# Second attention layer of a two-layer gated network: the inverse standard deviations by one GpSimd power instead of VectorE's Newton steps

## The reference, cut to what matters

```
def _layernorm(x, eps=1e-05):
    m, v = mean(x), var(x)                 # over the 256 features of a token
    return (x - m) / sqrt(v + eps)
...
x = x + tanh(g_ffn[0])   * _L0_ffn_ref(_layernorm(x), ...)                # 64 experts
x = x + tanh(g_xattn[1]) * _L1_xattn_ref(_layernorm(x), ctx, ctx, mask, ...)   # "first" norm
x = x + tanh(g_ffn[1])   * _L1_ffn_ref(_layernorm(x), ...)                # "second" norm
```

## Time and profile before

| what | value |
|---|---|
| time, median of 3 runs | 2185.94 us (2185.69 to 2190.29) |
| span of the profiled execution | 2056.7 us |
| what lies between that span and the median | 129.2 us |
| busy, share of the span: TensorE, VectorE, ScalarE, GpSimd | 90%, 77%, 60%, 44% |
| second attention layer in the trace | about 1138 to 1841 us |

### The profile page before, as it was taken

The page is one execution under the profiler, slowest core; times in us unless marked ns, Lnnn a source line. Parts: engine busy times, 40 slices in busy tenths (PEclk is TensorE's granted clock), DMA queues, the critical chain, the costliest instruction groups (busy, mean ns, idle before and its releaser), DMA issues.

```text
span 2056.7 us, 58130 instructions
## 1 busy us (share of the span) xinstructions
PE 1843.9 (90%) x21352; PEld 1494.5 (73%) x21488; DVE 1577.7 (77%) x6201; ACT 1236.8 (60%) x2555; POOL 902.1 (44%) x844
## 2 busy tenths in 40 slices
PE   4999999999999996499999699999999999958856
PEld 3898888888888885388888477777777777733334
DVE  4899999999999998444444677777777777769976
ACT  3676676676676672122222466666666666648877
POOL 1276666666666667577777100000000000005468
PEclk8999999999999998699999899999999999989978
DMA  9831221221111112499998211111111111003264
GB/s 233 224 117 57 58 60 51 62 77 47 50 51 45 49 36 79 133 224 213 219 218 151 63 40 40 40 40 40 41 35 38 40 40 41 17 24 154 93 243 166
DMA packets 183321, 187.69 MB, mean 91 GB/s; under 512 B 36946, under 2 KB 165749, under 8 KB 180992
## 3 DMA queue, kind: packets, MB, share of 16 engines
q1 hardware_dynamic: 135520, 142.30, 22.1%
q0 software_dynamic: 47520, 41.67, 11.0%
HBM read 103.33 MB, written 140.77 MB: 119 GB/s over the span
## 4 chain that ended last, share of the span: by engine, by line
PE 46%; DVE 32%; issue 9%; DMA 7%; POOL 3%; ACT 1%; SPq 1%; POOLq 0%; DVEq 0%; ACTq 0%
PE bank L423 11%; PE tiles L354 6%; DMA accumulator<-ye,tid 6%; DVE mt L786 6%; PE tiles L336 4%; PE bank L386 3%; PE bank L438 3%; PE tiles L330 2%; PE tiles L348 2%; DVE hmax L1610 2%; PE bank L458 2%; POOL accumulator L1400 2%; PE bank L469 2%; DVE h_ring L1603 2%; PE bank L371 2%
## 5 line engine op out<-in xcount | busy, mean ns | idle before, releaser
L1912 POOL DMA_INDIRECT expert_rows<-pay,idx x512 | 504.7, 986 | 246.0 <-issue 172.2
L1926 POOL TENSOR_TENSOR res<-res,bias 128x256 f32<-128x256 f32 x64 | 46.5, 726 | 611.9 <-ACT xn L629 611.9
L786 DVE TENSOR_REDUCE mt<-tiles 128x8 f32<-128x1024 f32 x256 | 300.8, 1216 | 8.4 <-PE tiles L336 8.2
L587 ACT ACTIVATE pt<-tiles 128x2048 f32<-128x2048 f32 x128 | 244.3, 1909 | 7.7 <-PE tiles L354 7.7
L609 ACT ACTIVATE qkp<-bank,qb,keep 128x128 f32<-128x128 f32 x512 | 209.3, 471 | 51.9 <-PE bank L423 51.9
L1400 POOL DMA_INDIRECT accumulator<-ye,tid x128 | 198.7, 1552 | 87.1 <-DMA accumulator<-ye,tid 38.2
L609 ACT ACTIVATE qkp<-bank,kb,keep 128x128 f32<-128x128 f32 x500 | 207.1, 482 | 0.0
L423 PE MATMUL bank<-xt,w_q 128*128 128x128 f32 x1024 | 164.5, 284 | 1.0 <-ACT xt L595 1.0
L354 PEld LDWEIGHTS tiles<-qm,qkp 32*128 32x128 f32 x4096 | 125.8, 186 | 52.4 <-issue 27.0
L354 PE MATMUL tiles<-qm,qkp 32*128 32x128 f32 x4096 | 150.2, 283 | 10.6 <-DVE mt L786 3.7
L336 PE MATMUL tiles<-qkp 32*128 32x128 f32 x4096 | 152.6, 285 | 6.2 <-ACT qkp L609 6.2
(11 more groups left out here) (265 smaller groups left out, 4289.4 us busy)
## 6 DMA issues: line engine op xcount, KB each, us to landing
expert_rows<-zt POOLq DMA_DIRECT2D x16, 1032.0 KB, 10.0
xr<-expert_rows SPq DMA_DIRECT2D x64, 258.0 KB, 4.2
cxax<-in_ctx SPq DMA_DIRECT2D x128, 128.0 KB
cxax<-accumulator SPq DMA_DIRECT2D x128, 128.0 KB, 2.2
hidden_away<-h_ring SPq DMA_DIRECT2D x8, 1536.0 KB, 5.1
res<-in_x SPq DMA_DIRECT2D x64, 128.0 KB
accumulator<-xa SPq DMA_DIRECT2D x64, 128.0 KB, 1.8
accumulator<-zt SPq DMA_DIRECT2D x64, 128.0 KB
```

What stands on the lines that cost most here:

```text
L587: nc.scalar.activation(pt[r % 2][:, :, :], tiles[:, :, :], ACT.Exp).then_inc(sem(sm("exp_done")), 1)
L786: last = nc.vector.tensor_reduce(mt[:, j, :].rearrange("p (i e c) -> p i e c", i=RT, e=2)[:, :, :, 0], tiles[:, :, 2 * j * P:2 * (j + 1) * ...
L1912: G.indirect_dma_start(out=xe[:, :], out_offset=bass.IndirectOffsetOnAxis(ap=idx[r][:, n:n + 1], axis=0), in_=pay[r][:, :], in_offset=None ...
```

## The change

For the second layer `NORM_STEPS` becomes 3. VectorE writes `var`, goes on to `shifted(m)`, and then waits for GpSimd's step before it writes `nmr`. GpSimd's loop gets, ahead of each bias addition, a wait for `var`, the two waits that guard `rstd` (formerly VectorE's), and one `tensor_tensor` with the operation `pow` of 128x2 elements that writes `rstd` = var to the power of -0.5. The loop runs six turns longer (70 in place of 64) to serve the last blocks' second norm. The first layer keeps its 13 steps.

```
-    NORM_STEPS = 13
+    NORM_STEPS = (13, 3)
...
+        minus_half = sb("minus_half", [P, 2])
...
-                act.wait_ge(sem(sm("rstd_step")), NORM_STEPS * (b + 1))
+                act.wait_ge(sem(sm("rstd_step")), NORM_STEPS[L] * (b + 1))
...
-                act.wait_ge(sem(sm("rstd_step")), NORM_STEPS * (b + PAIR[L] + 1))
+                act.wait_ge(sem(sm("rstd_step")), NORM_STEPS[L] * (b + PAIR[L] + 1))
...
                 st.mark(V.tensor_scalar(var[:, :], mv[:, :, 1], EPS, None, ALU.add))
                 yield
+                if L == 1:
+                    dve.wait_ge(sem("rstd_step_1"), NORM_STEPS[1] * s1 + 2)
+                    nc.vector.scalar_tensor_tensor(nmr[:, :], mv[:, :, 0], -1.0, rstd[:, :], ALU.mult, ALU.mult
+                                                   ).then_inc(sem("rstd_step_1"), 1)
+                    return
...
-                    norming(11)
+                    norming(1)
                     shifted(m)
-                    norming(2)
+                    norming(1)
...
+            G.memset(minus_half[:, :], -0.5)
...
-            for b in range(NB):
-                pool.wait_ge(sem("xn1_done_1"), b + 1)
-                G.tensor_tensor(row(b), row(b), bias[:, :], ALU.add).then_inc(sem("biased_1"), 1)
+            for s in range(NB + PAIR[1]):
+                pool.wait_ge(sem("rstd_step_1"), NORM_STEPS[1] * s + 1)
+                wait(pool, "xn1_done_1", min(s, NB))
+                wait(pool, "xn2_done_1", s - PAIR[1])
+                G.tensor_tensor(rstd[:, :], var[:, :], minus_half[:, :], ALU.pow).then_inc(sem("rstd_step_1"), 1)
+                if s < NB:
+                    pool.wait_ge(sem("xn1_done_1"), s + 1)
+                    G.tensor_tensor(row(s), row(s), bias[:, :], ALU.add).then_inc(sem("biased_1"), 1)
```

More of the change, by code:

```diff
@@ L861, in inverses @@
                 V = nc.vector
-                st = Steps(dve, sm("rstd_step"), NORM_STEPS, s1)
+                st = Steps(dve, sm("rstd_step"), NORM_STEPS[L], s1)
                 dve.wait_ge(sem(sm("stats_done")), s1 + 1)
```

## The result

The changed kernel takes 2179.29 us (2171.91 to 2182.55, 5 runs) against 2188.35 us (2185.69 to 2190.29, 5 runs) of the kernel before beside it: a ratio of 0.9948, interval 0.9929 to 0.9967. The forecast was 2177.9 us, 8.04 us less than before; the medians differ by 9.1 us, and 0.52% of 2188 us is 11.4 us, with 7 to 16 us by the interval. So the timed runs show that there is a gain and about how large it is; which part of the phase it comes from is read from the traces. One of the later timed runs of the changed kernel (c1_after) took 3695.0 us where the others took 2185 to 2199, and is left out of its ratio.

The account below looks back on a forecast made before the run. The prediction took TensorE to bound the full slots and latency the two ends. Filling 3.66 plus draining 4.38 us gave 8.04 us, so 2185.94 became 2177.9 us, with a range of 2173.5 to 2186.5 us.

Parts of the forecast that it names:

- The power's time: The 128x2 power on GpSimd, called p: taken as 0.6 us, with bounds of 0.12 and 2.77 us.
- 3q: Three times the gain of one bare chain, q = 2.04 - p = 1.44 us, within the sum 3.72 + 3q.
- The hops: Handing over from VectorE to GpSimd and back: 0.08 us each way, 0.16 us together.
- bare chain: Newton steps from `var` to `nmr` at the pipeline's ends, where TensorE has nothing: 2.20 us, each to gain 1.44 us.
- Filling: Start of the phase: first chain 1.44, wait for block 1's `xn` 0.61, second maximum 1.61; together 3.66 us gained.
- Full slots: The 59 middle slots: power hidden in slack, gain taken as 0, with 2.95 us as the other end.
- Draining: End of the phase: slot 65's wait for `qm` 1.18, head sums 0.32, two bare chains 2.88; together 4.38 us gained.
- what lies outside the span: Whole execution: 129.2 us between the profiled span and the measured median were said to lie outside and stay.
- start-up cost: Rival in the filling stretch: the first power runs code not run before, adding an extra L once; chance 0.05.
- the ends were not hidden: Denies the rival that expert-sum loads or feed-forward weights hold the chains at the ends: 2183 to 2186 us, chance 0.05.
- the power did not block VectorE's `qm`: Denies the rival that `shifted` (0.88 us) starts only when the power ends; its chance is within the slow power's 0.14.
- The slow power: Rival: a power over 2.71 us delays each full slot one for one; at 4 us some 2264 us; chance 0.14.

Follow-up runs that it names:

- e7: Changed kernel with the token maximum moved from between head norm and residual to the start of the slot; ratio 0.9934 to the kernel before.
- e9: Changed kernel with the token maximum at slot start and the second layer's copy of the values moved from ScalarE to VectorE; ratio 0.9914 to the kernel before.
- e1: Kernel before, all Newton steps still on VectorE, with only the order changed: `shifted` right behind `var`, the other twelve instructions after it; ratio 0.9992.
- e4: Changed kernel with the power kept, but VectorE waits for it ahead of `shifted`, undoing the new order; ratio 0.9936 to the kernel before.
- c0_before: Kernel before, unchanged, run again for a trace from an execution of known device time; ratio 0.9987.
- e3: Changed kernel with four spare GpSimd powers per call, each awaited, ahead of the one that counts; ratio 1.0314 to the kernel before.
- e6: Changed kernel with the power in the first layer too, on GpSimd behind each block's second scatter transfer; ratio 1.0173 to the kernel before.

## Why the prediction was right, and where it was off

**The power's time.** 0.6 us taken, 0.70 measured. This was a guess inside bounds of 0.12 and 2.77 us and not a derivation, and that it came so close is partly luck: the term 3q moves by three times its error. The prediction also counted ten instructions as removed from VectorE; it is eleven, which changes no term, since the chain was priced by its 2.20 us. The hops were 0.16 together by forecast; by the trace 0.15 and 0.03 in the fill, 0.07 and 0.04 in the drain. A bare chain gained 1.29 us in the fill and 1.40 in the drain, against 1.44.

**Filling**, 3.66 forecast, 4.2 between the two profiled executions. The first chain gave 1.29; L403 of block 1 came 2.10 us earlier, so that wait gave 0.81 for 0.61; the scores of block 1 came 2.56 us earlier and the second maximum 4.18, so the wait behind the Newton steps gave 1.62 for 1.61. The 0.46 us between 2.10 and 2.56 are mostly the clock: the first L336 took 2.09 us before and 1.68 after. TensorE's granted clock in this stretch differs between executions of one kernel, and the fill with it: 25.9 and 26.6 us before, 20.8 and 21.7 after. The 1 us kept open was the right size; it went either way.

**Full slots**, 0 forecast; 10.53 us a slot in both traces of before, 10.52 and 10.53 in the two of after, so nothing clear of scatter. Right in size. The reason given was incomplete: "the middle is TensorE's", and "ScalarE is no bound for it", which was read at `xn` alone. e7 shortened TensorE's wait at L372 and the slot did not move; e9 took 0.17 us out of ScalarE's round besides (5.21 to 5.04 us from L610 to the end of `copy_at`) and it did. The slot is a ring over both: in e7 5.1 us of TensorE from L387 to the end of L424 and 5.2 us of ScalarE from L610 to the end of `copy_at`, with two hops of 0.04 and 0.14 us. TensorE's 97% hid that, since it fills the ring's other half with work of its own. This was the step that failed in the reading, though it cost the forecast nothing.

**Draining**, 4.38 forecast; slot 65 gave 1.25 (1.18 forecast) and the tail 3.28 (0.32 + 2.88 forecast), together 4.53. The attribution was wrong in one term: 1.18 us were booked to the new place of `shifted`, but e1 shows the place alone worth nothing in sum and e4 the power alone worth 4.3. Slot 64 then took back 2.7 us in the one trace by the lower clock, which hit the kernel before in c0_before as well. What decides between the levels there stays open: the idle time before it is 2.5 to 2.6 us in each case (2.60 before and 2.48 in e4 and e7 at the higher level, 2.61 in c0 and 2.48 in after at the lower).

**The sum.** Without slot 64 the pieces give 4.2 in the fill, 0.6 in the 61 slots (which is within scatter) and 4.5 in the drain, 9.3 us, with it 6.6; the medians say 9.1. By the two traces of each kernel the phase fell by 6.6 to 11.9 us, clock included. The base of the forecast, 2185.94 us, carried the wrong statement of what lies outside the span; it did no harm only because the change leaves the first layer alone.

**The rivals.** No start-up cost (0.73 us for the first power); the ends were not hidden; the power did not block VectorE's `qm`, which took 0.88 us beside it as before. The second `var`, by contrast, took 0.48 us instead of 0.17 and ended with GpSimd's addition. The Trainium skill (SBUF — State Buffer, Who interferes with whom) states that a VectorE instruction with at most one SBUF input, outside the modes that use two ports, does not contend with GpSimd, and that a tensor_scalar can. The trace agrees: `qm` reads one tensor from PSUM and one from SBUF and was not slowed, `var` is a tensor_scalar and was. The slow power did not occur, and e3 showed that in the full slots it would have cost what was said.

## What to carry to other kernels

In a software pipeline read the slack of a full slot and the bare chains of its ends separately: eleven instructions less per slot on a 77% busy engine were worth nothing in 59 slots and about 9 us at the two ends, and eleven calls out of seventy would have done. Before a step goes to an idle engine, look at that engine's whole queue from its start, not only at its busy share (e6), and compute by how much the step may be late before the slot follows one for one (e3). A 97% busy engine need not be the bound: test it by taking one of its waits away, and if the slot stays, look for the ring that closes through another engine.

## What the runs showed that was not expected

A GpSimd power over two columns takes 0.70 us and an addition over 256 columns 0.73 us on the same engine. A program on one core had one execution whose first layer ran at 11.8 us a block, and all others in traces at 13.6 to 14.0 us; but for e6 the code there is the same. In all the longer ones VectorE's maximum waits 67 to 79 us in sum for what the profile calls "remote", in the trace of before not at all, and the cause stays open. Slot 64 of the drain took between 10.2 and 13.3 us in the kernels whose full slots take 10.5, by the granted clock.
